# Twelve row-maximum units moved into the last three chunks of stage one, and one tensor cleared by GpSimd instead of by DMA

## The reference

```python
xn = layernorm(x)
k, q, v = split(xn @ W_kqv + b_kqv)           # 16 heads of 16
attn = q @ k.T * 0.25 + slopes * tril(j - i), masked where j > i
y = softmax(attn) @ v @ W_proj + b_proj
logits = xn @ Wg; probs = softmax(logits)      # each of 8 experts takes its 512 best tokens
ffn[token] = weight * (gelu(xn @ W1[e], exact) @ W2[e])
out = x + y + ffn
```

## Time and profile before

| what | us |
|---|---|
| median of 3 runs | 676.47 (675.32 to 680.0) |
| profiled execution, its own time | 671.29 |
| span of its trace | 669.5 |
| busy in the span: TensorE | 532.4 (80%) |
| VectorE | 413.3 (62%) |
| GpSimd | 345.6 (52%) |
| ScalarE | 331.9 (50%) |

### The profile page before, as it was taken

The page is one execution under the profiler, slowest core; times in us unless marked ns, Lnnn a source line. Parts: engine busy times, 40 slices in busy tenths (PEclk is TensorE's granted clock), DMA queues, the critical chain, the costliest instruction groups (busy, mean ns, idle before and its releaser), DMA issues.

```text
span 669.5 us, 13130 instructions
## 1 busy us (share of the span) xinstructions
PE 532.4 (80%) x4383; PEld 314.5 (47%) x4383; DVE 413.3 (62%) x819; ACT 331.9 (50%) x623; POOL 345.6 (52%) x487
## 2 busy tenths in 40 slices
PE   1878488758888988979857879978776789999992
PEld 0445354324433544535423434433234668778782
DVE  3756334977999899898899977764212143233331
ACT  3464454205756666766635575756743323333330
POOL 4648110302634564555543388988835077655552
PEclk9999799978988999999979898989987889999997
DMA  5598788593232453444523265534895455454410
GB/s 165 168 265 121 249 261 262 167 301 95 86 99 72 117 160 101 137 121 124 155 62 98 77 179 150 178 117 128 284 315 110 98 122 135 116 106 115 93 44 9
DMA packets 104813, 96.44 MB, mean 144 GB/s; under 512 B 38625, under 2 KB 91937, under 8 KB 104741
## 3 DMA queue, kind: packets, MB, share of 16 engines
q1 hardware_dynamic: 94478, 74.02, 39.9%
q0 software_dynamic: 6576, 17.91, 9.0%
q10 hardware_dynamic: 3696, 3.67, 2.1%
HBM read 44.35 MB, written 40.05 MB: 126 GB/s over the span
## 4 chain that ended last, share of the span: by engine, by line
PE 32%; DVE 26%; POOL 15%; issue 8%; SPq 8%; DMA 5%; ACT 4%; POOLq 0%; DVEq 0%; ACTq 0%
DVE mx L869 11%; PE ps L1270 9%; PE ps L1283 7%; PE ps L1076 6%; POOL sorted_rows L596 4%; POOL pr_all L619 4%; POOL yn L589 3%; DVE mx L864 3%; PE ps L1148 2%; SPq L316 2%; PE ps L1129 2%; POOL w_low L583 2%; PE ps L1174 2%; SPq L407 2%; PE ps L1159 2%
## 5 line engine op out<-in xcount | busy, mean ns | idle before, releaser
L755 ACT ACTIVATE pr_all<-ps 128x512 f32<-128x512 f32 x320 | 182.5, 598 | 152.9 <-PE ps L1148 151.8
L869 DVE TENSOR_REDUCE mx<-ps 128x2 f32<-128x768 f32 (+1 forms) x192 | 155.8, 859 | 19.0 <-PE ps L1129 18.2
L619 POOL TENSOR_SCALAR_AFFINE_SELECT pr_all<-pr_all 128x384 f32<-128x384 f32 x128 | 64.6, 529 | 137.2 <-ACT pr_all L755 137.1
L1148 PE MATMUL ps<-qs,ks 128*128 128x512 f16 (+2 forms) x448 | 117.4, 334 | 14.7 <-ACT pr_all L755 6.3
L1129 PE MATMUL ps<-ks,qs 128*128 128x384 f16 (+3 forms) x512 | 117.5, 315 | 0.0
L1126 PE MATMUL ps<-maxmask,idb 128*128 128x256 bf16 (+1 forms) x320 | 84.6, 264 | 36.3 <-DVE mx L869 24.9
L1159 PE MATMUL ps<-pr_all,vt 128*17 128x512 f32 (+3 forms) x1024 | 86.3, 457 | 12.6 <-POOL pr_all L622 12.6
L1270 PE MATMUL ps<-pr_all,xnp 128*128 128x128 f16 x936 | 78.4, 227 | 3.2 <-DMA pr_all<-sorted_rows 3.0
L1148 PEld LDWEIGHTS ps<-qs,ks 128*128 128x128 f16 x448 | 38.9, 100 | 85.0 <-ACT pr_all L755 54.4
L1043 DVE TENSOR_TENSOR pr_all<-pr_all 128x512 f16<-128x512 f32 x39 | 27.0, 694 | 82.0 <-ACT pr_all L769 79.7
L1270 PEld LDWEIGHTS ps<-pr_all,xnp 128*128 x936 | 65.9, 99 | 15.1 <-issue 4.4
(11 more groups left out here) (173 smaller groups left out, 791.0 us busy)
## 6 DMA issues: line engine op xcount, KB each, us to landing
qs<-q_parts SPq DMA_DIRECT2D x64, 100.0 KB
ks<-k_parts SPq DMA_DIRECT2D x64, 96.0 KB
sorted_rows<-ecmp POOLq DMA_DIRECT2D x1, 5160.0 KB, 23.2
k_parts<-pr_all SPq DMA_DIRECT2D x16, 256.0 KB, 3.0
q_parts<-pr_all SPq DMA_DIRECT2D x16, 256.0 KB, 2.9
xr<-in_L_attn_x_dram SPq DMA_DIRECT2D x8, 512.0 KB, 4.2
w_h<-in_L_ffn_W_dram SPq DMA_DIRECT2D x16, 256.0 KB, 3.3
w_l<-in_L_ffn_W_dram SPq DMA_DIRECT2D x16, 256.0 KB, 3.0
```

The lines of the kernel that those rows point to most:

```text
L619: pool.affine_select(out=v, in_=v, compare_op=ALU.is_ge, fill=0.0, base=0, pattern=[[0, 3], [1, P]], channel_multiplier=-1).then_inc(sel_m ...
L755: act.activation(dst, src, ACT.Exp, scale=SCORE).then_inc(exp_made, 1)
L869: last = dve.tensor_reduce(mx[:, n1 % 2, :, 2 * g + c, t], ps[:, 2 * (u % 2):2 * (u % 2) + 2, c0:c0 + w], AX, ALU.max)
L1148: last = pe.matmul(out, ks[:, p, c, t * P:(t + 1) * P], rhs, start=True, stop=True, skip_group_check=True)
```

## The change

Units 0 to 11 of row 0 move into stage one: in chunks 5, 6 and 7 one unit stands ahead of each k or q product on TensorE, and its reduction ahead of that product's low half on VectorE. These units use banks 0 and 1 (shared with the transposes) and 6 and 7 (shared with v), so the transposes and the v products gain waits on `max_made`, and an odd unit waits for the chunk's earlier `v_used`. What TensorE waited for ahead of the first unit (rows, constants, zeros; `rows_ready`) now stands ahead of chunk 5.

In chunks 0 to 4 the transposes stand between the second and third v product instead of ahead of the first, and ScalarE copies the first two v products before the transposed rows. Of the two banks of transposed rows VectorE now copies one (except for chunk 0). GpSimd clears all of `qs` with four memsets ahead of its first `halves_of_rows`; the four clearing DMAs of SP go. The ALiBi rows' casts on GpSimd move from behind `halves_of_rows(4)` to behind `halves_of_rows(2)`, VectorE's `slope_parts` from the end of chunk 1 to the end of chunk 0, and SP's `alibi_rows` from ahead of chunk 4's stores to ahead of chunk 3's.

```diff
+EARLY_FROM = 5
+EARLY = 4 * (B - EARLY_FROM)
+EARLY_AT = lambda n, c: 4 * (n - EARLY_FROM) + c
+max_bank = lambda u: 6 * (u % 2) if u < EARLY else 2 * (u % 2)
...
-                sp.wait_ge(zeros, 64)
+                sp.wait_ge(zeros, 4)
...
                 if n == 1:
-                    zero_rows()
+                    sp.wait_ge(const_made, 11)
+                    sp.dma_start(qk_d[1][:, :, ROWS:QROWS, :].rearrange("b a r m -> (b a) (r m)"),
+                                 empty[0:2 * B, 0:S][:, None, :].broadcast_to([2 * B, 2 * NP, S])).then_inc(zrows_in, 16)
                 if n == 2:
                     constant_rows()
-                if n == 4:
+                if n == 3:
                     alibi_rows()
...
+            for p in range(2):
+                for e in range(2):
+
+                    pool.memset(qs[:, p, e].rearrange("r c n -> r (c n)").bitcast(F32), 0.0).then_inc(zeros, 1)
             halves_of_rows(0)
...
-                for a_ in range(2):
+                for a_ in range(1 if n else 2):
...
                 for c in range(4):
                     hi(c)
-                    if n < B - 1 and c == 2:
-                        take_rows(n + 1)
+                if n < EARLY_FROM:
+                    copy_v((0, 1))
+                if n < B - 1:
+                    take_rows(n + 1)
                 if n < B - 2:
                     root(n + 2)
...
+                copy_v((2, 3) if n < EARLY_FROM else range(TB))
...
                 for c in range(4):
+                    if n >= EARLY_FROM:
+                        row_max(0, EARLY_AT(n, c) // NU, EARLY_AT(n, c) % NU)
                     dve.wait_ge(hi_made, 4 * n + c + 1)
...
+                if n < B - 1:
+                    dve.wait_ge(t_made, n + 2)
+                    after(dve, v_made, 4 * n)
+                    dve.tensor_copy(xt[(n + 1) % 2][:, 1].rearrange("p k n -> p (k n)"), bank[1].bitcast(F16)).then_inc(t_used, 1)
+                if n == 0:
                     slope_parts()
...
+            for n in range(B):
+                pe.wait_ge(t_used, 2 * n + 2)
+                xt_n = xt[n % 2]
+                if n == EARLY_FROM:
+                    rows_ready()
+                for c in range(4):
+                    if n >= EARLY_FROM:
+                        if c % 2:
+                            pe.wait_ge(v_used, TB * n)
+                        max_unit(0, EARLY_AT(n, c) // NU, EARLY_AT(n, c) % NU)
+                    after(pe, lo_made, 4 * (n - 1) + c + 1)
...
+                if EARLY_FROM <= n < B - 1:
+                    pe.wait_ge(max_made, EARLY_AT(n, 2) + 1)
+                    turn_rows(n + 1)
+                if n >= EARLY_FROM:
+                    pe.wait_ge(max_made, EARLY_AT(n, 3) + 1)
+                for t in range(TB):
+                    if n < EARLY_FROM and t == 2:
+                        turn_rows(n + 1)
```

More of the change, by code:

```diff
@@ L547, in _ @@
             halves_of_rows(2)
+            pool.wait_ge(sl_made, 1)
+            for e in range(2):
+                mark(pool.tensor_copy(qs[0:3, e, 0], sl[0:3, 6, :].rearrange("p (c e) -> p e c", e=2)[:, e][:, :, None]
+                                      .broadcast_to([3, NP, S])))
+            pool.sem_inc(al_made, 2)
             halves_of_rows(3)
@@ L818, in _, with row_max @@
             measure(1)
+            def row_max(n1, g, k):
+                u = NU * (NG * n1 + g) + k
+                dve.wait_ge(sm_made, u + 1)
+                c0, b0 = 0, max_bank(u)
+                if k == NU - 1:
+                    last = dve.tensor_reduce(mx[:, n1 % 2, :, 2 * g:2 * g + 2, 1],
+                                             ps[:, b0:b0 + 2, :].rearrange("p e (c n) -> p e c n", c=2),
+                                             AX, ALU.max)
+                for c, t in UNITS[k][:0 if k == NU - 1 else None]:
+                    w = P * (t + 1)
+                    last = dve.tensor_reduce(mx[:, n1 % 2, :, 2 * g + c, t], ps[:, b0:b0 + 2, c0:c0 + w],
+                                             AX, ALU.max)
+                    c0 += w
+                last.then_inc(max_made, 1)
             def slope_parts():
@@ L1088, in turn_rows, with max_unit, rows_ready @@
                 last.then_inc(t_made, 1)
+            def max_unit(n1, g, k):
+                u = NU * (NG * n1 + g) + k
+                p1 = n1 % 2
+                if k == 0:
+                    pe.wait_ge(grp_in[p1][g], 64 * (n1 // 2 + 1))
+                after(pe, max_made, u - 1)
+                for e in range(2):
+                    dst, c0 = bank[max_bank(u) + e], 0
+                    ends = [P * (t + 1) for _, t in UNITS[k]]
+                    total, step = sum(ends), ends[-1]
+                    diag = dst[:, total - step * len(ends):total].rearrange("p (a n) -> p a n", n=step)[:, :, step - P:]
+                    pe.matmul(diag, idb[:, :], maxmask[:, None, :].broadcast_to([P, len(ends), P]),
+                              start=True, stop=False, skip_group_check=True)
+                    for (i, t), w in zip(UNITS[k], ends):
+                        last = pe.matmul(dst[:, c0:c0 + w], qs[:, p1, e, 2 * g + i, P * t:P * (t + 1)],
+                                         ks[:, p1, 2 * g + i, 0:w], start=False, stop=True, skip_group_check=True)
+                        c0 += w
+                last.then_inc(sm_made, 1)
+            def rows_ready():
+                pe.wait_ge(rows_in[0], 16 * 8)
+                pe.wait_ge(zeros, 4)
+                pe.wait_ge(rows_in[1], 32)
+                pe.wait_ge(rows_in[2], 16)
+                pe.wait_ge(const_made, 11)
             turn_rows(0)
@@ L1196, in turn_limits @@
                 pe.transpose(bank[7][:, 0:P], thr[:, 0:1].broadcast_to([P, P]), idf[:, :]).then_inc(prt_made, 1)
-            pe.wait_ge(rows_in[0], 16 * 8)
-            pe.wait_ge(zeros, 64)
             pe.wait_ge(xb_made, 1)
-            pe.wait_ge(rows_in[1], 32)
-            pe.wait_ge(rows_in[2], 16)
-            pe.wait_ge(const_made, 11)
-            for g in range(NG):
-                for k in range(NU):
-                    max_unit(0, g, k)
+            for u in range(EARLY, NG * NU):
+                max_unit(0, u // NU, u % NU)
             turn_max(0)
```

63 lines of the change are left out of this document (8 added, 55 removed).

## The result

| what | before | changed |
|---|---|---|
| median, us | 676.48 (675.32 to 680.0, 4 runs) | 668.0 (665.5 to 670.55, 4 runs) |
| profiled execution, us | 671.29 | 670.55 |
| busy in the span: TensorE / VectorE / GpSimd / ScalarE | 532.4 / 413.3 / 345.6 / 331.9 | 534.4 / 424.7 / 352.8 / 326.4 |
| first scores begin, in the trace | 151.44 | 146.03 |

A forecast was written before the change was run, and what follows sets the result against it. Limits up to the scores: ScalarE's copies and DMA in stage one, VectorE in row 0's maxima, then the shift rows' landing. Scores at 142.9 instead of 151.4, 8.5 us: 671.3 becomes 662.8, median 5.2 higher, 668.0; range 657 to 678.

The forecast's parts named there:

- The start: Ahead of the first cast: GpSimd's four memsets beside VectorE's normalising make the start 0.7 us later, between 0 and 1.2.
- Chunks 0 to 4: Stage one: the new order shrinks an undisturbed chunk from 10.54 to about 8.9 us; chunks 0 and 1 give 3.4 together.
- The first constant: SP's queue: without the zeros SP reaches the constants at 37.3 instead of 45.62, 8.3 us earlier; chunk 4 freed at 64.1.
- ALiBi and group 0: SP's queue ahead of chunk 5: ALiBi issue ends at 62.9, the wait takes 5.8 us, group 0 is there at 78.8.
- the second rival: Ahead of chunk 5: group 0 is there in time, TensorE goes on at 69.7, scores 132.3, 657 us; chance 0.15.
- Chunks 5 to 7: Stage one with four units each: 11.3, 11.4 and 11.0, sum 33.7 us, plus 1.5 lost to TensorE's slow clock.
- The last v product: End of stage one on TensorE: at 114.0 instead of 110.73, 3.3 us later, with 12 units done.
- SP's quarters: After stage one: SP sends the weights' quarters first, so shift rows are issued 21.9 us after the last v product, at 135.9.
- The landing: Shift rows, first issue to scores: 7 us, between 5.4 and 12.3, nearer the lower since the list has hardly begun.
- The scores: Row 0's first scores begin at 142.9 instead of 151.4, 8.5 us sooner.
- The first rival: Shift rows' landing: the list DMA holds them anyway, scores at 154.1, 2.7 us later than before, 679 us; chance 0.12.
- A sooner start is kept: Stages two and three, untouched: stage two's first row is VectorE's, 50.07 busy of 54.56 us, so an earlier start should be kept.

The follow-up runs named there:

- e3: Changed kernel without early units, all 20 units of row 0 behind stage one and the new chunk order in all eight chunks; ratio 0.987 to the kernel before.
- e4: Kernel before with only GpSimd's four memsets clearing qs at the start instead of SP's four clearing DMAs; ratio 0.9904 to the kernel before.
- e5: Changed kernel with SP's wait for the first two ALiBi DMAs, and the third DMA, moved behind group 0's four DMAs; ratio 0.9865 to the kernel before.
- again: Changed kernel, unaltered, run a second time on another chip (the second trace); 669.05 us against 675.91 for the kernel before, ratio 0.9906.
- e8: Changed kernel without early units and with row 0's shift rows issued behind the fifth weights' quarter instead of the sixth; ratio 0.9752 to the kernel before.
- e1: Changed kernel with row 0's shift rows issued behind the fifth weights' quarter instead of the sixth in SP's queue; ratio 0.9747 to the kernel before.
- e6: Changed kernel with SP's ALiBi wait behind group 0's DMAs and row 0's shift rows behind the fifth weights' quarter; ratio 0.9732 to the kernel before.
- e2: Changed kernel with GpSimd's 5160 KB list DMA issued in row 0's third group instead of ahead of row 0; ratio 0.9831 to the kernel before.
- e9: Changed kernel without early units, ALiBi wait later, shift rows behind the fifth quarter, list DMA behind the shift rows' landing; ratio 0.9759 to the kernel before.
- e10: Changed kernel with all twelve early units, ALiBi wait later, shift rows behind the fifth quarter, list DMA behind their landing; ratio 0.9725 to the kernel before.
- e11: Changed kernel with four early units (chunk 7 only), ALiBi wait later, shift rows behind the fifth quarter, list DMA behind their landing; 682.38 us against 704.62, ratio 0.9697.

## Why the prediction was right, and which terms were off

The total was right, 8.5 us by the medians. The steps on the way:

1. **The start**: 0.7 forecast (0 to 1.2), 0.97 measured. The memsets took 7.03 us and VectorE's normalising beside them 2.35 instead of 1.38. The Trainium skill, page "SBUF — State Buffer", section "Who interferes with whom", has the shared port pair as the cause, with the loser blocked for the whole instruction. The trace agrees: the first of the four instructions ends at 9.56, just behind the memset's end at 9.40, and the other three run at their usual pace. The cost was not the 1.8 of a whole memset, since the last one was already 0.56 us under way when VectorE came.
2. **Chunks 0 to 4** at 8.9: right; 8.77 between transposes where nothing waits (57.67 to 66.44 in the changed kernel, and in chunks 5 to 7 of e3). VectorE's copy of its bank took 0.69 instead of 1.4, and TensorE's wait for `halves_of_rows(3)` was 2.30 instead of 1.5; both were hidden.
3. **The first constant** at 37.3, measured 39.32, 2.0 late. Chunk 4's release followed, 66.16 against 64.1. With the zeros gone but the chunks in their old order the two were 40.65 and 67.45 (e4), so the new order gave 1.3 here and not the 3.4 that I took for two chunks. The chain of waits shows where it went. From 28.3 on it runs over VectorE, which now copies its bank and does `slope_parts` (1.9 us) ahead of chunk 1's work, so the last low half ended at 37.17 and not at 36.3. All four low halves then came at once, and SP needed 2.15 us for their stores, where I had allowed 1. Chunk 2's last store had been issued by 65.01 instead of 61.4, since from the first constant to it SP needed 25.7 us and not 24.1.
4. **ALiBi and group 0**: the pair's issue ended at 66.50 instead of 62.9, SP's wait was 4.5 (2.2 in the second trace) instead of 5.8, and group 0 was there at 80.79 (77.74) instead of 78.8. SP's wait as the cause was right. What I had not asked is what comes next: e5 shows that it is the third ALiBi DMA, for with SP's wait moved away the first unit stood only 1.2 us sooner. TensorE's readiness for chunk 5, put at 69.7, was 74.39: chunk 4 ended 8.2 us behind ScalarE's release, where I had allowed 5.6 without a reason. That was hidden behind group 0, but the second rival was priced on it.
5. **Chunks 5 to 7**, 35.2 with the clock: 36.6. TensorE is the bound in chunk 6, 11.44 of 11.45. The clock after the wait was 0.50, the lower of its two levels (1.2 of 2.4 GHz), until 84.91, so 4.1 us of work at half speed and 2.1 lost instead of 1.5. Before, it rose at 81.56, 3.0 us after the work had begun at 78.55.
6. **The last v product** at 114.0: 117.4, which is 3.4 late: 2.0 from step 4, 1.4 from step 5.
7. **SP's quarters**, 21.9 from the last v product: **17.4**, the term that failed most. I took over the distance of the kernel before. But there SP was itself behind: it issued groups until 108.8 and chunk 7's stores only until 113.5, 2.7 after the last v product, and the x load at 116.40. Now VectorE's last low half begins at 114.39, its store follows at once, and the x load goes out at 117.76, 0.35 after the last v product instead of 5.7. From that load to the last weights' load it is 16.4 before and 16.6 now. This error and the former nearly cancel: the shift was issued at 134.85, for 135.9.
8. **The landing**, 7 of the range 5.4 to 12.3: **11.2** and 11.4, near the upper end. I reasoned that a list which has hardly begun can't hold the rows. The runs show another rule, in us from the shift's issue to the scores: 12.3, 11.2, 11.4, 11.4, 12.5, 12.4 and 9.7 where the list was issued 7.3, 1.4, 1.4, 1.4, 1.4, 5.6 and 0.14 us ahead (before, changed, again, e5, e3, e4, e8); 5.2 and 5.6 where it was 1.07 and 0.9 us behind (e1, e6), 3.8 without it (e2). In e1 and e6 TensorE was still at row 1's units; the landing itself ended after 3.75 us, as in e2, e9, e10 and e11, so my lower bound of 5.4 was too high.

   The DMA records of the traces show what decides. The list's first data follow its issue by 2.8 to 4.0 us. In the six kernels with a landing of 3.75 all 128 records of the shift started ahead of them. In the slow ones 0 (before, e4), 4 (e3), 6 (again), 17 (e5), 20 (changed) and 85 (e8) did, and even the 43 that e8 had left took until 134.4, 5.3 us from the list's first data.

   The Trainium skill, page "DMA: Bandwidth & Descriptors", section "Queues, rings and completion order", lets each DMA engine take the queues in turn, packet by packet. If a packet were one record of the trace, the shift would lose little, by an estimate about 2 us: 8 records per engine if 16 engines share the 128, each behind one record of the list of 0.20 to 0.26 us (122 to 164 of them in 2 us, on 16 engines). It lost 6 to 9. But the page gives about 9 to 17 descriptors as a typical packet, and the traces don't show where a packet ends, so the runs speak against my reading of the rule, and not against the rule.
9. **The scores**: 142.9 forecast, 146.03 and 143.58 measured; the lead in the traces 5.4 and 7.9, for 8.5. The first rival, that the list holds the shift rows anyway, had its mechanism right and only its place wrong: I had made it depend on an issue as late after stage one as before, which step 7 took away. It would have given 154.1. (Its 679 stands as 678 in the range.)
10. **A sooner start is kept**: mostly. The lead at the issue of the shift rows of rows 1 to 4 was 5.3, 6.1, 5.5 and 4.9 us and from the fifth on 2.7 to 3.2; in the second trace 7.7, 8.0, 7.3 and 6.6, then 4.8 to 5.3. About 2 us go in the fifth row, in both; what takes them there I have not tried to find. For e6 the lead falls there from 16.9 to 14.2.

What the twelve units as such did is the lesson that the total hides. I counted on 13.8 us less for VectorE behind stage one and got 13.9. But the way to the scores had three gates, TensorE's end of stage one, SP's quarters and the list, and the units made the first one 18.6 us later than in e3. By the scores' starts the zeros gave 4.4 (e4), and all the rest of the change together a further 1.0 or 3.5. Without the units, and with the new order in all eight chunks, the rest gave 5.4 (e4 to e3). Of the 8.0 us by which stage one ends sooner there, 4.5 come in chunks 5 to 7, where the changed kernel hasn't the new order. So the units, with the order that they displace, took 1.9 to 4.4 back.

Left open: how much of the 1.9 to 4.4 us is the units' own; whether the chunks' order or the ALiBi rows' place gave more of the 5.4; why the ALiBi pair lands in 2.2 us one time and 4.5 another; and whether a wait of TensorE for group 0 would go if the constants were sent in a form that lands quicker, which wasn't tried.

## What to carry to other kernels

Work moved ahead of a gate pays only if the gate's last arrival is that work: list all that the gated instruction waits for (here the maxima, a hand-written SP queue and a transfer) and move the latest first; sending the shift one quarter earlier in SP's queue, a change of one line, brought the ratio from 0.9865 to 0.9732 on one chip (e5 to e6), as much again as the whole change had brought. When work is pulled into an earlier stage, put it only where its inputs have landed without a wait: by the scores' starts four units in the last chunk beat twelve in three, 129.56 against 133.33. And take a distance from the trace before only after asking which engine was late in it, since a queue's backlog that the change removes goes out of that distance too.

## What the hardware did that I had not expected

- Four transfers of 8 KB on SP's queue land 3.75 us after their first issue if all their records start ahead of the data of a 5160 KB transfer on GpSimd's queue, and 9.7 us after it if a third of them don't (e8, issued 0.14 us behind the large one). The cost is a step, hardly a slope: issued 1.4 us behind, the way to the scores is 11.2 to 12.5, and 7.3 behind it is 12.3.
- A GpSimd memset that only writes SBUF slows VectorE's work on SBUF: of four TENSOR_SCALAR of 128x256 f32 the first took 1.39 us beside it, 0.41 without, and ended 0.16 behind the memset.
- TensorE's granted clock stood at 0.50 for the first 4.1 us of work after 6.4 us of waiting, and before for the first 3.0 us after 8.75 idle: more idle time did not mean a longer slow start.
- On two of the chips the same stretch, from row 7's shift to the end, took 233 to 240 us instead of 213 to 215, while the marks up to the end of stage one were the same within 3 us in kernels that are the same up to there.
